# Attention of a GAT layer with its output turned, P scaled by its row sums on GpSimd, and ELU read from PSUM

## What is computed

```
h   = relu(layernorm(x))
Wh  = h @ W[head];  e = leaky_relu(f1[:, None] + f2[None, :]);  e = where(adj > 0, e, -1e9)
h'  = elu(softmax(e) @ Wh)            # for each of the 4 heads, then concatenated
out = elu(the same with W_out, a_out, one head over all 1024 features)
y   = relu(out @ w1 + b1) @ w2 + b2 + out
x   = x + layernorm(y) * gamma + beta
g   = relu(layernorm(x))
x   = x + deg * (g @ Wi.T + b) + adj @ (g @ Wj.T)
```

## Time and profile before

| | |
|---|---|
| median of 3 runs | 1540.99 us (1539.92 to 1544.33) |
| the profiled execution | 1542.53 us, its span 1540.7 us |
| PE busy | 1428.9 us, 93% of the span |
| DVE busy | 1136.4 us, 74% |
| ACT busy | 1066.9 us, 69% |
| POOL busy | 236.3 us, 15% |
| mean granted clock of TensorE | 0.974 |

### The profile page before, as it was taken

One profiled execution on the slowest core, in us unless ns is written; L12 is line 12 of the kernel. 1 busy time (PEld: TensorE's weight loads), 2 busy tenths in 40 slices (PEclk: granted clock), 3 DMA queues, 4 the chain that ended last, 5 costly groups with the idle time before them and its releaser, 6 DMA issues.

```text
span 1540.7 us, 28639 instructions
## 1 busy us (share of the span) xinstructions
PE 1428.9 (93%) x10792; PEld 1333.2 (87%) x10792; DVE 1136.4 (74%) x2836; ACT 1066.9 (69%) x1700; POOL 236.3 (15%) x254
## 2 busy tenths in 40 slices
...
GB/s 170 14 1 28 2 15 1 42 2 28 15 28 15 15 28 2 42 1 29 15 29 14 2 41 1 29 15 28 15 2 42 2 30 14 28 2 25 5 28 14
DMA packets 30056, 33.04 MB, mean 21 GB/s; under 512 B 1248, under 2 KB 28896, under 8 KB 29792
## 3 DMA queue, kind: packets, MB, share of 16 engines
...
## 4 chain that ended last, share of the span: by engine, by line
PE 81%; ACT 8%; DVE 7%; issue 3%; DMA 0%; POOL 0%; POOLq 0%; DVEq 0%; ACTq 0%
PE psA L736 52%; PE psR L789 8%; PE psT L890 4%; PE psT L814 4%; PE psA L848 4%; PE psA L859 4%; ACT ff L389 2%; ACT arg L420 1%; DVE hx_lo L577 1%; PE psT L780 1%; ACT prob_hi L426 1%; ACT hx_hi L441 1%; PE psT L768 1%; DVE arg L609 1%; PE psT L747 1%
## 5 line engine op out<-in xcount | busy, mean ns | idle before, releaser
L736 PE MATMUL psA<-whx_hi,prob_hi 128*128 128x258 f32 x1024 | 303.4, 296 | 14.2 <-DVE fcol L588 13.6
L736 PE MATMUL psA<-whx_hi,prob_lo 128*128 128x258 f32 x1024 | 291.0, 284 | 0.0
L736 PE MATMUL psA<-whx_lo,prob_hi 128*128 128x256 f32 x1024 | 289.9, 283 | 0.0
L577 DVE TENSOR_TENSOR prob_lo<-psR,prob_hi 128x1024 fp32r<-128x1024 f32 x160 | 195.2, 1220 | 55.5 <-ACT prob_hi L426 55.3
L356 POOL TENSOR_SCALAR elu_ex<-elu_in 128x512 f32<-128x512 f32 x160 | 103.4, 646 | 854.1 <-ACT elu_in L432 702.1
L609 DVE CUSTOM_DVE_ANT_0 arg<-psT,mask 128x512 f32<-128x512 f32 x320 | 208.0, 687 | 27.4 <-PE psT L780 24.4
L416 ACT ACTIVATE arg<-arg,fcol 128x512 f32<-128x512 f32 x320 | 212.5, 714 | 18.0 <-DVE gmax L609 18.0
L420 ACT ACTIVATE arg<-arg,nmax 128x512 f32<-128x512 f32 x320 | 212.0, 712 | 10.5 <-DVE nmax L620 10.5
L736 PEld LDWEIGHTS psA<-whx_hi,prob_hi 128*128 128x128 f32 x1024 | 195.8, 191 | 23.0 <-issue 17.8
L736 PEld LDWEIGHTS psA<-whx_hi,prob_lo 128*128 128x128 f32 x1024 | 194.9, 190 | 4.9 <-issue 3.6
L736 PEld LDWEIGHTS psA<-whx_lo,prob_hi 128*128 128x128 f32 x1024 | 195.6, 191 | 0.0
...
## 6 DMA issues: line engine op xcount, KB each, us to landing
...
```

Source lines behind the costliest of these rows:

```text
L577: return dve.tensor_tensor(out=dst, in0=src, in1=hi.bitcast(fp32), op=ALU.subtract)
L736: i = pe.matmul(o, a, b_, start=(k == 0), stop=(k == n - 1))
```

## The change

- The heads' attend has Wh as the standing operand and P as the moving one, so its result comes out with features on the partitions, as mix2 wants it. turn2 goes, on PE, ACT and DVE, and so does `hcat`. BACK's attend is as before. All its matmuls move 256 columns; the column of ones is gone.
- The sum of a row of P comes from the accumulator of the exp (`accum_out`, ACT). A new step rinv on DVE takes its reciprocal, a new step scale on POOL multiplies P by it (two instructions of 128x512), and turn_p waits for that instead of for the exp.
- elu_in goes. elu_low is a DVE instruction of 128x512 that reads PSUM, elu_exp stays, and elu_out takes the result from PSUM a second time; psA is held until elu_out is done. New steps hx (ACT, a copy of 128x512) and hx_lo (POOL, a subtraction of 128x512) split the result for mix2. elu_low waits until hx_lo of the unit two before it is done.
- b2 is added to `out` by POOL (add_b2, 128x1024); the four bias matmuls of ffn2 go, and DVE's ffn2 waits for add_b2.
- In the setup W_out, a_out, b_gc and b2 are loaded behind the first batch, and the split of W_out is made behind the first unit.
- All five tables are written anew: other orders, and other lateness of the steps. turn_in is 1 late (0 before), conv 4 (3 before).

Of the tables only two lines stand here; the rows below show the orders.

```diff
-    ("elu_in", 5, 2), ("norm_in", 0, 0), ("elu_out", 4, 2), ("elu_out", 5, 2), ("conv", 0, 3), ("probs", 7, 1),
+    ("rowmax", 9, 2), ("rinv", 8, 2), ("elu_low", 5, 3), ("probs", 7, 2), ("elu_out", 5, 3), ("elu_low", 6, 2),
...
-            def elu_low_(c):
-                pool.wait_ge(elu_xa, c.unit + 1)
-                pool.wait_ge(elu_xd, c.unit + 1)
-                wait(pool, elu_out, c.unit - 1)
-                pool.tensor_scalar(elu_ex[:, c.buf, :, :], elu_in[:, c.buf, :, :], 0.0, -3.0e38, ALU.min, ALU.max).then_inc(elu_low, 1)
+            def scale(c):
+
+                pool.wait_ge(rinv_made, c.unit + 1)
+                for n in range(2):
+                    i = pool.tensor_scalar(arg[:, c.abuf, n, :], arg[:, c.abuf, n, :], rinv[:, c.abuf, n:n + 1], None, ALU.mult)
+                i.then_inc(p_scaled, 1)
+
+            def hx_lo_(c):
+                pool.wait_ge(hx_hi, head_unit(c.b, c.h, c.u) + 1)
+                pool.tensor_tensor(out=hx[1][:, 2 * c.h:2 * c.h + 2, c.u * HN:(c.u + 1) * HN], in0=elu[:, c.buf, :, :],
+                                   in1=hx[0][:, 2 * c.h:2 * c.h + 2, c.u * HN:(c.u + 1) * HN].bitcast(fp32), op=ALU.subtract).then_inc(hx_lo, 1)
+
+            def add_b2(c):
+                if c.b == 0:
+                    pool.wait_ge(ld[LD_B2], 16)
+                pool.wait_ge(o_turned, c.b + 1)
+                pool.tensor_tensor(out=wk[:, :, :], in0=wk[:, :, :], in1=b2_bc[:, None, :].to_broadcast([P, NC, F]),
+                                   op=ALU.add).then_inc(b2_added, 1)
...
-                    i = act.activation(a[:, n, :], a[:, n, :], ACT.Exp, bias=nmax[:, c.abuf, n:n + 1])
+                    i = act.activation(a[:, n, :], a[:, n, :], ACT.Exp, bias=nmax[:, c.abuf, n:n + 1], accum_out=rsum[:, c.abuf, n:n + 1])
...
-            def turn2(c):
-                act.wait_ge(m2_turned, NC * c.b + c.info + 1)
-                wait(act, m2_done, NC * c.b + c.info - 1)
-                act.activation(hx[c.info % 2][0][:, :, :], psT[:, :, :].rearrange("p a n -> p (a n)").rearrange("p (k n) -> p k n", k=OC),
-                               ACT.Copy).then_inc(hx_hi, 1)
+            def hx_(c):
+                act.wait_ge(elu_out, c.unit + 1)
+                wait(act, m2_done, NC * (c.b - 1) + 2 * c.u + 2)
+                act.activation(hx[0][:, 2 * c.h:2 * c.h + 2, c.u * HN:(c.u + 1) * HN], elu[:, c.buf, :, :], ACT.Copy).then_inc(hx_hi, 1)
...
+            def rinv_(c):
+                dve.wait_ge(arg_exp, c.unit + 1)
+                dve.reciprocal(rinv[:, c.abuf, :], rsum[:, c.abuf, :]).then_inc(rinv_made, 1)
+
+            def elu_low_(c):
                 dve.wait_ge(att_done, c.unit + 1)
-                dve.reciprocal(rec[:, c.buf, :], psA[c.pair][:, :, F]).then_inc(elu_rec, 1)
-                dve.wait_ge(elu_rec, c.unit + 1)
-                dve.tensor_scalar(elu_in[:, c.buf, 1, :], psA[c.pair][:, 1, 0:F], rec[:, c.buf, 1:2], None, ALU.mult).then_inc(elu_xd, 1)
+                if c.unit > 1:
+                    b, h, u = units[c.unit - 2]
+                    if h != BACK:
+                        dve.wait_ge(hx_lo, head_unit(b, h, u) + 1)
+                dve.tensor_scalar(elu[:, c.buf, :, :], psA[c.pair][:, :, 0:F], 0.0, -3.0e38, ALU.min, ALU.max).then_inc(elu_low, 1)
...
-                dve.scalar_tensor_tensor(out=dst, in0=elu_ex[:, c.buf, :, :], scalar=-1.0, in1=elu_in[:, c.buf, :, :],
+                dst = wk[:, 2 * c.u:2 * c.u + 2, :] if c.h == BACK else elu[:, c.buf, :, :]
+                dve.scalar_tensor_tensor(out=dst, in0=elu[:, c.buf, :, :], scalar=-1.0, in1=psA[c.pair][:, :, 0:F],
                                          op0=ALU.add, op1=ALU.max).then_inc(elu_out, 1)
...
             def turn_p(c):
-                pe.wait_ge(arg_exp, c.unit + 1)
+                pe.wait_ge(p_scaled, c.unit + 1)
...
+                        terms = [(whx[:, j, c.h, part], whl[:, j, c.h, part], prob[0][:, c.buf, j, :], prob[1][:, c.buf, j, :]) for j in range(NC)]
+                    r = product(psA[c.pair][:, n, 0:F], terms)
                 r.then_inc(att_done, 1)
-                lend((c.pair,), (elu_xa, c.unit + 1), (elu_xd, c.unit + 1))
+                lend((c.pair,), (elu_out, c.unit + 1))
...
-                    pe.matmul(y, pick[:, 1, :], brow[:, :], start=True, stop=False)
                     for k in range(KC):
-                        i = pe.matmul(y, midT[:, k, n * P:(n + 1) * P], w2_sb[:, k, :], start=False, stop=(k == KC - 1))
+                        i = pe.matmul(y, midT[:, k, n * P:(n + 1) * P], w2_sb[:, k, :], start=(k == 0), stop=(k == KC - 1))
```

More of the change, by code:

```diff
@@ L7 @@
 SP_STEPS = [
[L8 removed]
+    ("load", 0, 0), ("store", 0, 4), ("load_back", 0, 3),
 ]
 PE_STEPS = [
[L11 removed]
[4 rows of a table removed]
[L16 to L18 removed]
@@ L20 @@
+    ("turn_p", 6, 2), ("attend", 5, 3), ("turn_p", 7, 2), ("attend", 6, 2), ("turn_p", 8, 2), ("turn_gc", 0, 4),
+    ("attend", 7, 2), ("turn_out", 0, 3), ("conv_in", 0, 4), ("conv_in", 1, 4), ("attend", 8, 2), ("turn_p", 9, 2),
+    ("ffn1", 0, 3), ("turn_in", 0, 1), ("attend", 9, 2), ("mix2", 0, 2), ("mix2", 1, 2), ("m1", (0, 0), 1),
+    ("m1", (0, 1), 1), ("m1", (1, 0), 1), ("m1", (1, 1), 1), ("conv", 0, 4), ("m1", (2, 0), 1), ("f2rows", 0, 1),
 ]
 ACT_STEPS = [
-    ("args", 9, 1), ("turn_out", 0, 2), ("probs", 8, 1), ("elu_in", 6, 1), ("elu_in", 7, 1), ("elu_exp", 6, 1),
@@ L23 @@
-    ("ffn1", 0, 2), ("elu_exp", 7, 1), ("elu_in", 8, 1), ("probs", 9, 1), ("elu_exp", 8, 1), ("norm_in_out", 0, 0),
-    ("turn2", 0, 1), ("turn2", 1, 1), ("elu_in", 9, 1), ("elu_exp", 9, 1), ("turn_in", 0, 0), ("norm_ff_out", 0, 2),
[3 rows of a table removed]
-    ("turn_gc", 0, 2), ("args", 2, 0), ("f2rows", 2, 1), ("elu_in", 0, 0), ("probs", 2, 0), ("args", 3, 0), ("args", 4, 1),
-    ("elu_in", 1, 0), ("conv_in", 0, 2), ("probs", 3, 0), ("elu_exp", 0, 0), ("f2rows", 1, 0), ("args", 5, 1),
-    ("elu_in", 2, 0), ("probs", 4, 1), ("conv_in", 1, 2), ("elu_exp", 1, 0), ("elu_exp", 2, 0), ("args", 6, 0),
@@ new lines @@
+    ("probs", 4, 3), ("args", 6, 2), ("hx", 2, 2), ("probs", 5, 3), ("elu_exp", 3, 2), ("args", 7, 2), ("elu_exp", 4, 3),
+    ("probs", 6, 2), ("hx", 3, 2), ("args", 8, 2), ("probs", 7, 2), ("norm_gc_out", 0, 4), ("elu_exp", 5, 3),
+    ("turn_gc", 0, 4), ("elu_exp", 6, 2), ("probs", 8, 2), ("args", 9, 2), ("elu_exp", 7, 2), ("turn_out", 0, 3),
+    ("conv_in", 0, 4), ("hx", 6, 2), ("conv_in", 1, 4), ("norm_in_out", 0, 1), ("probs", 9, 2), ("hx", 7, 2),
+    ("elu_exp", 8, 2), ("hx", 8, 2), ("ffn1", 0, 3), ("turn_in", 0, 1), ("elu_exp", 9, 2), ("mix2", 0, 2), ("m1", (0, 0), 1),
@@ L33 @@
+    ("m1", (0, 1), 1), ("m1", (1, 0), 1), ("m1", (1, 1), 1), ("m1", (2, 0), 1), ("f2rows", 0, 1), ("hx", 9, 2),
+    ("m1", (2, 1), 1), ("args", 0, 1),
 ]
 DVE_STEPS = [
-    ("x2", 0, 3), ("m1", (0, 1), 1), ("turn2", 3, 2), ("m1", (1, 0), 1), ("m1", (1, 1), 1), ("f2rows", 0, 1),
-    ("m1", (2, 0), 1), ("rowmax", 0, 1), ("rowmath", 0, 1), ("rowmax", 1, 1), ("rowmath", 1, 1), ("norm_gc", 0, 3),
-    ("m1", (2, 1), 1), ("rowmax", 2, 1), ("norm_gc_out", 0, 3), ("mix2", 1, 2), ("probs", 0, 1), ("rowmax", 3, 1),
@@ L48 @@
-    ("turn2", 2, 1), ("m1", (0, 0), 0),
+    ("m1", (1, 0), 2), ("m1", (1, 1), 2), ("f2rows", 0, 2), ("conv", 0, 5), ("m1", (2, 0), 2), ("rowmax", 0, 2),
+    ("norm_in_out", 0, 1), ("rowmath", 0, 2), ("rowmax", 1, 2), ("rowmath", 1, 2), ("rowmax", 2, 2), ("rinv", 0, 2),
+    ("m1", (2, 1), 2), ("rowmath", 2, 2), ("rinv", 1, 2), ("mix2", 1, 3), ("rowmax", 3, 2), ("f2rows", 2, 3),
+    ("probs", 0, 2), ("rowmath", 3, 2), ("ffn2", 0, 4), ("rinv", 2, 2), ("norm_ff", 0, 4), ("m1", (3, 0), 2),
+    ("rowmax", 4, 3), ("norm_ff_out", 0, 4), ("probs", 1, 2), ("rowmath", 4, 3), ("m1", (3, 1), 2), ("elu_low", 0, 2),
```

191 lines of the change are left out of this document (87 added, 104 removed), and 7 rows, old and new, of tables (ACT_STEPS, PE_STEPS).

## The result

The changed kernel takes 1683.6 us (median, 1681.0 to 1685.8), the kernel before 1540.8 in the same series: a ratio of 1.092, 95% interval 1.090 to 1.095. The prediction had the direction, but 1581 us for the size, and its range ended at 1625.

What follows compares the result with a forecast made beforehand. DVE's dense stretch, with blocking by POOL, was to bound it: PE's 84.0 + 3.5 waiting + 5.0 blocking = 92.5 us a round; 37 + 150 + 13 x 92.5 + 190 + 2 = 1581 us, range 1510 to 1625.

Steps and rivals of the forecast that it cites:

- The price of the scale: POOL's scale, 20 instructions a round at 0.62 us each, part of 32.3 us of POOL a round.
- POOL becomes part of the chain: Rival: scale takes up to hx_lo's 1.18 us, turn_p waits for it; 98 us a round, 1655 us; chance 0.09.
- PE is spared: PE's work in a steady round: turn2 3.2, ffn2's bias matmul 1.1, fewer columns 0.15; together 4.4 us less.
- the bias: PE's bias matmuls of ffn2, whose removal was to spare 1.1 us a round.
- The forecast's 84.0: PE alone would need 84.0 us a steady round after the change.
- PE busy about 1360 us: Sign expected if the forecast held: PE's busy time over the kernel.
- DVE and ACT a round: Busy time in a steady round: DVE 67 us (less 1.5 of blocking), ACT 64.
- The dense stretch and the blocking: Turn_p 0 to attend 7: DVE short, 3.5 us of waiting; POOL blocks DVE's SBUF instructions, 5.0 more; 92.5 a round.
- it adds in full: POOL's 5.0 us of blocking lengthens each round by all of it, DVE being the limit in the stretch.
- its last rival: More is blocked than DVE instructions with two SBUF inputs; called small, inside the range, no chance of its own.
- The ends: Outside the 13 steady rounds: start stays 37, two lighter rounds 150 instead of 170, tail 190 instead of 184 us.
- The clock was left at 1.00: PE's granted clock in steady rounds stays at 1.00, with PE busy 91% of a round.

Runs made afterwards that it cites:

- e6: The change with scale written as mult by the reciprocal's column and then add 0.0, in place of mult alone; same result: 1590.8 us (1.031).
- e5: The change plus 63 POOL instructions of 128x512 behind its last round, other engines idle, to price operations: mult by constant 1.50 us, by column 1.56, mult and add 0.62.
- e8: The change with scale as mult 1.0, add 0.0 (P not divided) and POOL's three 128x1024 passes cut to 128x8: 1529.4 us, 0.991 of before.
- e4: The kernel before without ffn2's bias matmuls, with one 128x1024 addition on POOL (beta added, b2 left out): 1542.6 us, ratio 0.9999.
- e11: e6 with POOL's b2 addition moved earlier, behind hx_lo of unit 8, beside DVE work that reads PSUM: 1576.2 us (1.023).
- e13: e11 with beta's and gamma's passes on DVE, beta's behind rinv 1, x2 behind elu_out 1, gamma alone ahead of probs 3: 1565.5 us (1.015).

## Why the prediction was wrong

By its own steps:

- **The price of the scale is the step that failed.** "POOL: scale 20 x 0.62" took the price from L356, which has the same instruction and shape and another pair of operations. It measured 1.57 (median). As a term: 20 x 0.95 = 19 us of POOL a round (51.4 instead of 32.3, whose terms add up to 32.4), of which 5.4 came out as time (97.3 against 91.9 in e6). Between the two profiled executions, 1679.0 and 1590.0, that is 13 x 5.4 = 70 of 89 us; 14 more lie ahead of the third batch (206.05 against 192.32) and 5 in the tail (208.0 against 203.1). The price has to be taken for the operations, not for the shape.
- **The chance went with it.** The rival "POOL becomes part of the chain" is what happened, with its sign (turn_p waits for scale); it had 0.09 and was left out of the range, although the text had said that L356 has two constants, and scale one operand from SBUF. Its upper bound, 1.18 from hx_lo, was no bound: hx_lo is a tensor_tensor instruction, and measures 1.28 itself. That its round of 98 us is near the 97.3 measured is luck: it was worked out for a scale of 1.18. On a straight line between e6 (0.69 us, 91.9) and the change (1.57, 97.3), an estimate, 1.18 us make a round of 94.9. And the step from constants to a column, which the rival named, isn't what costs: 1.50 and 1.56 in e5.
- **PE is spared: too much.** 4.4 us a round were forecast; PE's busy time falls from 87.6 to 84.7 in e8, by 2.9. The forecast's 84.0 comes close to 84.7 only because it was taken from the whole round, with its 0.8 us of waiting. Of the 1.5 too much, 0.7 is the bias (0.43 us a round in e4, not 1.1); the rest was not taken apart. And the reading that the round of before is PE's alone was too simple, as e4 shows. The sign "PE busy about 1360 us" was missed even at the forecast's price: 1398.7 in e6, 1410.4 in the change.
- **DVE and ACT a round: near.** The forecast for DVE was 67 less 1.5 of blocking, 65.5; e8, with the least blocking, has 64.2. ACT has 64.8 for 64. elu_low costs 0.60 us from its start to the next (785.21 to 785.81 in e6; its median length is 0.69), where 0.65 was taken; exp's sum is a separate instruction on ACT, 0.19 us long, and the next one starts 0.09 after it (744.60 and 744.69 in the change), where 0.1 was taken.
- **The dense stretch and the blocking: shown as a mechanism, near in size partly by luck.** e6 gives 91.9 for 92.5, with DVE named in 4.9 us of PE's waiting a round. The wide passes take 5.0 us from DVE in one of its rounds where 5.0 was forecast (with those of the scales 5.7), but "it adds in full" was too much: without the passes the round is 4.0 shorter. e8 has 87.8 for 87.5, and there the terms are others than forecast: PE's 84.7 and 3.4 of waiting, of which 0.4 and not 3.5 names DVE. And e11 shows that moving one pass changes a round by 1.1 us. elu_out stayed at a median of 0.68, as forecast. The Trainium skill's "SBUF — State Buffer", section "Who interferes with whom", also names copy and cast among DVE's instructions that can take the shared pair, which the prediction left out of its count (its last rival, "small", has more blocked than it counted, and names neither). The trace agrees (the cast L619 took 1.41 us in place of 0.17).
- **The ends.** Head 150 for two lighter rounds: in e6 153.9 (38.44 to 192.32), in the change 168, as the scale stands there too. Tail: 190 from the last turn_in was too little. In e6 it is about 204 by the same measure, where the kernel before had 184.0. These 14 us too many and the head's 4, less 13 x 0.6 for the rounds, are the 10 us between e6 and the forecast. Which of the tail's waits makes it up was not tried.
- **The clock was left at 1.00, and it isn't.** In the kernel before, the granted clock of TensorE is 1.00 in each of the thirteen rounds. In the change it is 0.98 in eleven of them and 1.00 in two, in e6 0.98 in seven, in e8 1.00 in all. Two rounds of e13, one after the other:

```profile
367.41:458.19 90.78, 86.16 (x640) 80.07 (x639) 67.15 (x169) 64.29 (x122) 31.07 (x33) 0.98 0.06 19
458.19:547.62 89.43, 85.02 (x640) 78.58 (x638) 67.18 (x169) 64.07 (x122) 31.10 (x33) 1.00 0.06 19
```

In the first the clock is at its lower level, 1.2 GHz, for some 3.4 us from 425.3 on, right behind turn_p 5 (424.29), for which PE had waited 2.19 us; in the second, with the same wait, it stays at 2.4 GHz. Why is open. The round costs 1.3 us more. In the change there is no such difference (but for the first, 97.0 to 98.6 us at 0.98, and 97.0 and 97.4 at 1.00), so the clock has no visible part in the 103 us; in e6 its rounds at 0.98, but for the first, are 0.4 to 1.5 us longer than the 91.7 of the others, some 5 us in all.

e13's full round is 89.4 us at a clock of 1.00, with PE busy 85.0; the rest is its waits, 2.2 for prob_lo of DVE and 1.3 for ACT's copy of f2 above all. What stays open is whether an order without them exists: taking prob_lo's away in one place only moved it, and ACT's queue, which now has a part, was not varied.
